# Queries and keys first, scores behind: two blocks of TensorE's steps trade places

## The reference

```
x = x + L0_attn(norm(x))      # one head, causal
x = x + L0_xattn(norm(x), ctx)
x = x + L0_ffn(norm(x))       # 8 experts, each takes its best 128 tokens
x = x + L1_attn(norm(x))      # 16 heads of 64, causal: the part that is changed
x = x + L1_xattn(norm(x), ctx)  # 16 heads of 8, softmax over the 32 largest of 77 scores
x = x + L1_ffn(norm(x))       # 8 experts, top 2 per token
```

```
q, k, v = x @ w_q, x @ w_k, x @ w_v            (per head)
weights = softmax(causal(q @ k.T) / sqrt(64))
out     = concat_heads(weights @ v) @ w_o
```

## Time and profile before

| | |
|---|---|
| median of 3 runs | 603.25 us (600.56 to 604.59) |
| the profiled execution | 600.98 us, its span 599.2 us |
| mean granted TensorE clock | 0.98 |
| TensorE (matmul) busy | 529.7 us, 88% of the span |
| VectorE, ScalarE, GpSimd busy | 397.8, 303.7, 223.2 us |
| steps of the self-attention | from about 149.85 to 408 us of the span |

### The profile page before, as it was taken

The page is one execution under the profiler, slowest core; times in us unless marked ns, Lnnn a source line. Parts: engine busy times, 40 slices in busy tenths (PEclk is TensorE's granted clock), DMA queues, the critical chain, the costliest instruction groups (busy, mean ns, idle before and its releaser), DMA issues.

```text
span 599.2 us, 12139 instructions
## 1 busy us (share of the span) xinstructions
PE 529.7 (88%) x3968; PEld 414.7 (69%) x3968; DVE 397.8 (66%) x2194; ACT 303.7 (51%) x760; POOL 223.2 (37%) x227
## 2 busy tenths in 40 slices
PE   4878769997899899988999888978898899999997
PEld 2566336874667657677777566767677778999997
DVE  3575774634332597966497999985968798744643
ACT  2242314334786566765675556745775555322222
POOL 5015840001433445753356535552733433340000
PEclk9997899999999999999899999989999999999999
DMA  4600011424000000000000000001520000010000
GB/s 125 194 1 15 28 40 36 121 73 158 2 1 1 1 2 1 2 2 2 2 1 2 2 0 2 2 2 59 189 66 10 15 15 19 19 32 1 28 1 10
DMA packets 23064, 19.17 MB, mean 32 GB/s; under 512 B 2055, under 2 KB 18523, under 8 KB 23003
## 3 DMA queue, kind: packets, MB, share of 16 engines
q1 hardware_dynamic: 22491, 17.36, 9.4%
q0 software_dynamic: 512, 1.05, 0.6%
HBM read 15.38 MB, written 3.01 MB: 31 GB/s over the span
## 4 chain that ended last, share of the span: by engine, by line
PE 60%; DVE 20%; ACT 9%; issue 6%; POOL 3%; DMA 1%; DVEq 0%; ACTq 0%; POOLq 0%
PE ps L1803 51%; DVE wk L1161 4%; PE ps L2199 4%; DVE top L1151 3%; DVE nmax L1103 3%; ACT w_mem L1555 2%; PE ps L2261 2%; ACT prT L1568 2%; DVE sel_mem L994 2%; POOL xs_dram L770 1%; DVE xn L1124 1%; PE ps L2453 1%; PE ps L1815 1%; DVE xn L838 1%; DVE bn L825 1%
## 5 line engine op out<-in xcount | busy, mean ns | idle before, releaser
L1103 DVE TENSOR_REDUCE nmax<-ps 128x2 f32<-128x256 f32 (+1 forms) x64 | 51.2, 820 | 61.2 <-PE ps L1803 59.2
L1161 DVE MATCH_REPLACE8 wk<-top,wk 128x77 f32<-128x77 f32 x384 | 80.5, 223 | 0.0
L687 POOL TENSOR_TENSOR w_mem<-w_mem,rinv 128x256 f32<-128x256 f32 (+3 forms) x44 | 53.1, 1218 | 51.3 <-DVE rinv L1109 50.7
L1282 DVE TENSOR_TENSOR sel_mem<-gr,ps 128x512 f32<-128x512 f32 x47 | 32.2, 686 | 47.2 <-ACT gr L1745 46.4
L1745 ACT ACTIVATE gr<-ps 128x512 f32<-128x512 f32 x47 | 28.1, 598 | 62.2 <-PE ps L1803 62.2
L1151 DVE MAX8 top<-wk 128x8 f32<-128x77 f32 x384 | 57.9, 223 | 0.1
L1803 PE MATMUL ps<-cat_mem 64*128 64x256 f32 (+7 forms) x276 | 55.6, 476 | 1.5 <-ACT cat_mem L1539 1.5
L1555 ACT ACTIVATE w_mem<-ps,nmax 128x128 f32<-128x128 f32 (+3 forms) x88 | 44.5, 520 | 11.5 <-DVE nmax L1103 11.5
L716 POOL TENSOR_SCALAR wk<-wk 128x616 f32<-128x616 f32 x16 | 28.1, 1753 | 58.2 <-DVEq L1165 57.8
L1803 PE MATMUL ps<-prT,cat_mem 128*64 128x128 f32 x640 | 42.9, 282 | 1.9 <-DVE x L1186 1.4
L611 POOL TENSOR_TENSOR rstd<-var_eps,minus_half 128x4 f32<-128x4 f32 x8 | 8.2, 1025 | 94.7 <-DVE var_eps L831 94.6
(11 more groups left out here) (348 smaller groups left out, 1356.5 us busy)
## 6 DMA issues: line engine op xcount, KB each, us to landing
w_mem<-in_L_ffn_W_dram SPq DMA_DIRECT2D x12, 256.0 KB, 3.2
f_mem<-in_L_ffn_Wg_dram SPq DMA_DIRECT2D x8, 256.0 KB, 2.8
f_mem<-in_L_ffn_Wu_dram SPq DMA_DIRECT2D x8, 256.0 KB, 3.1
f_mem<-in_L_ffn_Wd_dram SPq DMA_DIRECT2D x8, 256.0 KB, 3.8
sel_mem<-in_L_ffn_W_dram SPq DMA_DIRECT2D x4, 256.0 KB, 4.2
xs_dram<-zero SPq DMA_DIRECT2D x1, 960.0 KB, 6.2
ys_dram<-f_mem SPq DMA_DIRECT2D x15, 64.0 KB, 1.5
xs<-xs_dram SPq DMA_DIRECT2D x3, 256.0 KB, 3.3
```

What stands on the lines that cost most here:

```text
L687: pool.tensor_tensor(pr[s][:, :, at:at + n], pr[s][:, :, at:at + n], rinv[:, i % 8, :].unsqueeze(2).to_broadcast([P, 2, n]), ALU.mult)\
L1103: dve.tensor_reduce(nmax[:, i % 8, :], ps[:, 2 * s:2 * s + 2, at:at + (c + 1) * P], X, ALU.max, negate=True).then_inc(nmax_ready, 1)
L1161: dve.match_replace(wk[q][:, t, h, :], top[q][:, t, h, 8 * r:8 * r + 8], src[:, t, h, :], GONE).then_inc(top_step, 1)
L1282: dve.tensor_tensor(hg[s][:, :], gr[s][:, :], ps[:, 2 * s + 1, :], ALU.mult)\
```

## The change

In each step the call of the scores moves from ahead of the projection of queries and keys to behind it. The arithmetic, the operands, the banks, the semaphores and the streams of the other engines stay as they are. `scores(U + 2)` still comes ahead of `queries`, `project_v`, the cross-attention pieces and `turn`. The projection's wait for `ptc_ready` moves with it and now stands ahead of the scores.

```diff
             for U in range(NU):
                 n, r = piece_of(U)
-                if U + 2 < NU:
-                    scores(U + 2)
                 for j in range(3, 4 * NP):
                     if U == FIRST[j] - 3:
                         if U:
                             pe.wait_ge(ptc_ready, U)
                         project_qk(j, 4)
                         taken = j + 1
+                if U + 2 < NU:
+                    scores(U + 2)
                 for k in range(3):
                     if U == STAGE[k + 1] + 3:
                         seven = queries(k, spare, *seven)
```

## The result

| | before | after |
|---|---|---|
| median | 602.55 us (600.56 to 604.59, 4 runs) | 627.19 us (623.94 to 629.89, 4 runs) |
| ratio of the runs | | 1.041 (95%: 1.036 to 1.047) |
| profiled execution, its span | 600.98, 599.2 | 623.94, 622.2 |
| mean granted clock of the profiled execution | 0.98 | 0.97 |

The kernel became 4.1% slower: 24.6 us on the medians, 22.96 us on the two profiled executions. The forecast was 616.3 with a range of 609 to 621. The direction was right; the time lies above the range.

What follows compares the result with a forecast made beforehand. TensorE and ScalarE were taken as nearly full in steps 0 to 5, VectorE as pacing 325 to 408 us. Stage 0 +6.4, stages 1 and 2 +5.5, stage 3 +1.2 make +13.1: 614.1 profiled, 616.3 median, range 609 to 621.

Steps and rivals of the forecast that it cites:

- the ring: Per step: projection, scores, row maxima, exponentials, copy of the transposes, next projection; 5.62 us, or 5.70 with a values' projection.
- The 0.73 us: Idle time of TensorE ahead of the transposes of step 2, at 161.22; claimed to vanish with the new order.
- the 5.2 us of waits: TensorE's waits listed as "issue", 11 times in the whole self-attention; the copy of the projection would be hidden.
- stage 0: Steps up to 10 with their output projection: +6.4 us, from +4.1 to +8, handed on whole to what follows.
- steps 20 to 30: Five projections in a row at steps 21 to 25, then steps 28 to 29, and the later transposes: +4.25 us.
- the half clock: Rival: waits bring 1.2 GHz stretches in the first steps, doubling projection and scores in two or three; +5, 621 us; chance 0.08.
- stage 1's single steps: Every second step has a projection; later scores cost 0 to 0.82 us in each of two steps, +1.0 in all.
- steps 31 to 47: Step 31 +1.0, vanished waits ahead of two output projections -0.8, later scores where VectorE idled in stage 3 +1.2: +1.4 us.
- which spans two steps: Old order: scores, row maxima, exponentials, copy, next projection reach over two steps, as the next scores precede the wait.
- only stage 0 pays: Rival: cross-attention pieces leave slack in later steps, so the loss is +4 to +8, 607 to 611 us; chance 0.14.
- faster: Rival: ScalarE's copy of the transposes is in time, only vanished waits count, -7 us, 596 us; chance 0.04.
- no effect: Rival: the projection was rarely what TensorE waited with; 603 us; chance 0.02.

## Why the forecast was too low

**Right.** The mechanism, the ring and its length: 5.72 and 5.85 us against 5.62 and 5.70. The 0.73 us and the 5.2 us of waits went. The waits moved to the projection, released by the copy of the transposes (1.3 to 2.1 us each, where about 1.1 was forecast), and ScalarE now waits for the row maxima (1.64 us). The delay is handed on whole. Step 28 to 29 was forecast at 5.62 and measured 5.71 with the new order in steps 21 to 29 only. At full clock stage 0 comes to 10.35 - 3.3 = 7.05 us (forecast 6.4), and steps 20 to 30 to 4.5 (4.25).

**Wrong: the clock left out of the sum.** The forecast put the half clock down as a rival with a chance of 0.08 and +5 us in stage 0. It came in the first turn of the ring or just ahead of it, in every execution profiled with the new order there. It took 3.3 us in stage 0, 1.5 in step 28 and 1.8 behind the last norm, 6.6 in all. Of these only the half clock in stage 0 comes with the change in every profile. The extra stretch of step 28 falls in step 24 in the run on steps 21 to 29 and is absent in the run with bank 7 and the new order, and the 1.8 are not shown to be the change's. What speaks for it stood in the working: a new wait of about 1 us in every step, ahead of the very matmuls of the ring. That belonged in the main case, as part of each wait's price; with what it measured the sum is 13.1 + 6.6 = 19.7. The rival's own +5 was about the right size: it gave 621 where its chance was put at 0.08.

**Wrong in size: stage 1's single steps.** The term was +1.0 from "the ring spans two steps there and mostly fits"; the trace has +3.35. The forecast let the later row maxima cost in two steps only, at most 0.82 us each. In the trace the delay grows in every step from 13 to 17, by 0.3 to 0.7, and by 0.7 again in step 20: VectorE has top-k work between the row maxima in program order, and late scores are not made up there. With less top-k the delay at step 18 fell from 2.9 to 1.6. The remaining terms (steps 31 to 47, +2.1 against +1.4) and the setup (-0.7) nearly cancel.

**Wrong, with little effect on the number: the slack of the old order.** The forecast called the old path one "which spans two steps". The copy made twice shows a ring of one step, 3.97 and 4.69 us, by the order of ScalarE's own queue. The forecast's sum didn't need it, as it took the old steps from the trace. It is why the new waits were paid in full. Two readings in the working are off as well, and carry no term: the busy share of the lengthened steps is 73% (23.98 of 26.77 x 22.64 / 18.54) and not 75, and the scores ahead of the projection at 163.81 took 1.0 us and not 1.2.

**On the numbers.** 13.05 forecast, +2.35 for the single steps, +0.65 and +0.25 for the rings, +0.7 for steps 31 to 47, -0.7 setup and 6.6 clock give 22.9, the measured difference of the profiled pair (22.96). On medians it is 24.6; the other runs of the kernel after have lower mean clocks (0.959 to 0.964) than the profiled one (0.970). The rival "only stage 0 pays" is refuted by the runs on steps 21 to 29 and on the single steps, "faster" and "no effect" by the result.

## What to carry to other kernels

Before a block is moved past a wait, write down the ring that the wait closes through every engine's program order, with the previous use of the bank in it, and do the same for the old order, since what looks like slack may be the bound already. Where two tiles share a bank, another bank removes the wait (here -0.6%), and another order only moves it (+4.1%). Where an order adds waits of a microsecond per step to TensorE, put its lower clock into the main sum and not among the rivals.

## What the hardware showed beyond that

The kernel before, unchanged, ran between 598.2 and 607.0 us over 23 runs on one chip, with mean granted clocks from 0.983 down to 0.963. The seven runs above 606 us all have 0.963 to 0.966, and the five up to 600.1 have 0.977 to 0.983. So a difference of half a per cent took a dozen runs and the trace to be seen. And a wait for several things misled: the 0.73 us at 161.22 is given to GpSimd, and it went when the transposes of stage 0 no longer waited for ScalarE's copy of the projection. The 5.2 us of "issue" are the same in the kernel with bank 7 in stage 0, and gone in the kernel after, so they lie in the later stages and end with this copy too.
